# A fused decoder layer on one core: one head in four turned on VectorE and through DRAM instead of on TensorE

## The reference

```
x1  = x  + attention(LN1(x), LN1(x), LN1(x), mask 256x256)      # 16 heads of 32
x2  = x1 + attention(LN2(x1), ctx, ctx, mask per sequence)      # keys and values from ctx
x3  = x2 + gelu(LN3(x2) @ w1 + b1) @ w2 + b2                    # 512 -> 2048 -> 512
out = x3 + batchnorm(W @ y(x3, ctx))                            # non-local block, 128 channels

attention: softmax(q k^T / sqrt(32) * mask - 10000 (1 - mask)) v, then an output projection
```

## Time and profile before

| | |
|---|---|
| median of 3 runs | 2041.2 us |
| lowest, highest | 2039.52, 2042.16 us |
| span of the profiled execution | 2038.2 us |
| busy: PE / DVE / ACT / POOL | 2018.1 / 1447.7 / 1166.7 / 450.6 us |
| granted clock of TensorE, mean | 0.997 |
| DMA | 332469 packets, 190.25 MB; q1 32.5% of 16 engines' span |

### The profile page before, as it was taken

The page is one execution under the profiler, slowest core; times in us unless marked ns, Lnnn a source line. Parts: engine busy times, 40 slices in busy tenths (PEclk is TensorE's granted clock), DMA queues, the critical chain, the costliest instruction groups (busy, mean ns, idle before and its releaser), DMA issues. The chain is left out here.

```text
span 2038.2 us, 41730 instructions
## 1 busy us (share of the span) xinstructions
PE 2018.1 (99%) x14096; PEld 1621.0 (80%) x14096; DVE 1447.7 (71%) x3874; ACT 1166.7 (57%) x3239; POOL 450.6 (22%) x434
## 2 busy tenths in 40 slices
PE   9999999999999999999999999999999999999998
PEld 8877777777777777777777776788888888888887
DVE  7798988888889888888888898565344443435333
ACT  4388888888888888787788888522111121212111
POOL 1011111111113242222232233053031331313000
PEclk9999999999999999999999999999999999999999
DMA  8513243243144344344334334432212212121201
GB/s 270 171 35 77 83 119 77 64 113 97 48 141 133 109 134 109 85 121 126 86 111 123 95 108 120 138 99 70 80 33 77 46 62 72 41 77 46 64 24 47
DMA packets 332469, 190.25 MB, mean 93 GB/s; under 512 B 210688, under 2 KB 276864, under 8 KB 332288
## 3 DMA queue, kind: packets, MB, share of 16 engines
q1 hardware_dynamic: 332288, 187.97, 32.5%
HBM read 137.00 MB, written 50.86 MB: 92 GB/s over the span
## 5 line engine op out<-in xcount | busy, mean ns | idle before, releaser
L1279 ACT ACTIVATE A_p<-A_p,A_nmax 128x256 f32<-128x256 f32 x1024 | 509.1, 506 | 0.0
L1564 DVE TENSOR_TENSOR A_p<-A_sc,A_mk 128x1024 f32<-128x1024 f32 x256 | 312.7, 1221 | 109.1 <-PE A_tp L1046 108.9
L1574 DVE CUSTOM_DVE_ANT_0 A_p<-A_p,A_ma 128x256 f32<-128x256 f32 x1024 | 374.5, 423 | 5.2
L1285 ACT ACTIVATE A_pt<-A_tp 128x512 f32<-128x512 f32 x512 | 276.9, 592 | 142.2 <-PE A_tp L1046 141.8
L1046 PEld LDWEIGHTS A_tp<-A_ident,A_p 128*128 128x128 f32 x2048 | 230.1, 141 | 71.8 <-issue 44.1
L1046 PE MATMUL A_tp<-A_ident,A_p 128*128 128x128 f32 x2048 | 274.2, 277 | 2.0 <-ACT A_pt L1285 1.6
L1279 ACT ACTIVATION_READ_ACCUMULATOR A_p<-A_p,A_nmax 128x1 f32 x1024 | 202.8, 198 | 0.0
L1414 ACT ACTIVATE A_mk<-A_tp,A_cols 128x512 f32<-128x512 f32 x62 | 42.7, 689 | 269.0 <-PE A_tp L68 269.0
L766 POOL TENSOR_TENSOR A_res<-A_res,A_o_bias 128x512 f32<-128x512 f32 x64 | 84.9, 1338 | 473.1 <-DVE A_nmax L1574 281.3
L1414 ACT ACTIVATE A_ma<-A_tp,A_cols 128x512 f32<-128x512 f32 x62 | 42.8, 690 | 242.4 <-PE A_tp L68 242.4
L66 PE MATMUL A_banks<-A_xt_h,A_w_h 128*128 128x512 f32 x384 | 161.3, 420 | 0.9 <-DVE A_res L1543 0.5
(11 more groups left out here) (245 smaller groups left out, 4856.4 us busy)
## 6 DMA issues: line engine op xcount, KB each, us to landing
A_x<-x SPq DMA_DIRECT2D x96, 256.0 KB, 3.6
A_res<-x SPq DMA_DIRECT2D x64, 256.0 KB, 2.9
A_rt<-inverses SPq DMA_DIRECT2D x512, 32.0 KB, 1.8
x<-A_res SPq DMA_DIRECT2D x64, 256.0 KB, 3.2
turned<-A_x SPq DMA_DIRECT2D x240, 64.0 KB, 2.3
inverses<-A_turned_inv SPq DMA_DIRECT2D x512, 1.0 KB
A_e<-ctx_t SPq DMA_DIRECT2D x16, 512.0 KB, 3.9
A_xt_l<-turned SPq DMA_DIRECT2D x16, 512.0 KB, 4.0
```

The lines of the kernel that those rows point to most:

```text
L1279: act.activation(p[:, g % 2, j, t, :], p[:, g % 2, j, t, :], ACT.Exp, scale=-1.0, bias=nmax[:, g % 2, j, t:t + 1], accum_out=rsum[:, g % 2 ...
L1285: act.activation(pt[:, j, :, :], tp[:, j % 2, :].rearrange("p (c s) -> p c s", c=TPB), ACT.Copy)\
L1564: dve.tensor_tensor(p[:, g % 2, heads, :, :].rearrange("p j t s -> p j (t s)"), sc[:, heads, :], m, ALU.mult)\
L1574: dve.tensor_tensor_reduce(out=a_, in0=a_, in1=ma[:, b, t, :], scale=-1.0, scalar=BIG, op0=ALU.add, op1=ALU.min, accum_out=nmax[:, g % 2, ...
```

## The change

MOVED = 1 head of each group, head 0, is no longer turned by TensorE. VectorE transposes its exponentials in 32x32 blocks in place (`exponentials_in_blocks`, one instruction of 128x512, in the slot in which they are made, after `scaled`). SP then writes them to a DRAM tensor in four DMAs, each of 32 partitions by 16 blocks of 32 floats (`store_exponentials`, between `store_inverses` and `load_inverses`), and at the start of the next slot reads them back with keys on the partitions in one DMA of 256 KB (`load_exponentials`, in runs of 128 floats), once the product that last read `pt` is done. TensorE turns heads 1, 2 and 3: two at the slot's start, one inside the first unit; `weigh` waits for the load as well. The first half of the mask now waits for the stores of the slot before, and for one turned head in place of two. ScalarE makes the first two exponentials at the slot's start, ahead of the copies, and has three copies in place of four. In `weighed` it now adds the bias into `cx` in place and then rounds `cx` into `ct_h`, two instructions; the lower part `ct_l` is made by GpSimd, after `until_maxima`, and no longer by VectorE.

```diff
+MOVED = 1
+TURNS = HPG - MOVED
...
@@ -538,6 +541,28 @@
+            def store_exponentials(r, h):
+
+                grp, _, g = group(r, h, 0)
+                sp.wait_ge(p_blk, grp + 1)
+                wait(sp, ld_p, (grp - 1) * DMA)
+                keys = p_dram[g % 2].rearrange("j t (b i) q -> i (j t b) q", i=32)
+                for n in range(P // 32):
+                    rows_ = slice(n * 32, (n + 1) * 32)
+                    own = p[rows_, g % 2, 0:MOVED, :, :].rearrange("i j t (b q) -> i (j t b) q", q=32)
+                    sp.dma_start(keys[:, :, rows_], own).then_inc(st_p, DMA)
+
+            def load_exponentials(r, h, pv):
+
+                grp, _, g = group(r, h, -1)
+                if grp == 0:
+                    sp.wait_ge(w_lo, 3 * KT)
+                else:
+                    sp.wait_ge(done, pv[1])
+                sp.wait_ge(st_p, (grp + 1) * (P // 32) * DMA)
+                sp.dma_start(pt[:, 0:MOVED, :, :].rearrange("p j a (b q) -> p (j a b) q", q=P),
+                             p_dram[g % 2].rearrange("j t (c p) q -> p (j t c) q", p=P)).then_inc(ld_p, DMA)
@@ -596,10 +621,14 @@
 
             def slot(r, k, h, a_, b_, own, pv):
                 if own:
+                    load_exponentials(r, h, pv)
                     store_inverses(r, h)
                     if h == 6 and 0 < k < NU:
                         for t in range(2):
                             load_res(k - 1, r - 1, t + 2)
+                if exists(k, h, 0):
+                    store_exponentials(r, h)
+                if own:
                     load_inverses(r, h)
...
+            def weighed(r, k, h):
+                grp, _, g = group(r, h, -2)
+                b, f = g // KT, g % KT
+                part = slice(b * S, (b + 1) * S)
+                wait_apart(pool, c_hi, grp + 1)
+                pool.tensor_tensor(ct_l[:, f, part], cx[:, :], f32(ct_h[:, f, part]), ALU.subtract).then_inc(c_lo, 1)
@@ -849,6 +885,8 @@
                     upper_context(k + 1, r + 1, 2)
                 if h != 2 or 0 < k < NU:
                     until_maxima(r, k, h)
+                if exists(k, h, -2):
+                    weighed(r, k, h)
...
-            def turn(r, k, h, j):
+            def turn(r, k, h, i):
                 grp, _, g = group(r, h, -1)
-                if NG * k + h - LAG - 1 == 0 and j == 0:
+                n, j = grp * TURNS + i, MOVED + i
+                if grp == 0 and i == 0:
                     pe.wait_ge(pgt_ok, B)
                     pe.wait_ge(m1_ok, B)
                 pe.wait_ge(exped, grp * HPG * TPB + (j + 1) * TPB)
-                wait(pe, pt_ok, grp * HPG + (j - 1))
-                if j < 2 and h in (0, 7) and k == (h == 0):
-                    pe.wait_ge(x_lo, (r + (h == 7)) * TT + (j + (3 if h == 0 else 1)))
+                wait(pe, pt_ok, n - 1)
+                if i < 2 and h in (0, 7) and k == (h == 0):
+                    pe.wait_ge(x_lo, (r + (h == 7)) * TT + (n % 2 + (3 if h == 0 else 1)))
                 for t in range(TPB):
                     for c in range(TPB):
-                        last = pe.transpose(tp[:, j % 2, c * S + t * P:c * S + (t + 1) * P],
+                        last = pe.transpose(tp[:, n % 2, c * S + t * P:c * S + (t + 1) * P],
                                             p[:, g % 2, j, t, c * P:(c + 1) * P], ident[:, :])
                 last.then_inc(turned, 1)
+            def turned_keys(j, c):
+
+                return pt[:, j, :, c * P:(c + 1) * P] if j < MOVED else pt[:, j, c, :]
 
             def weigh(r, h, bank):
                 grp, blk, g = group(r, h, -1)
                 b, f = g // KT, g % KT
                 occupy(bank, cx_ok, NG, h - LAG, r)
-                pe.wait_ge(pt_ok, (grp + 1) * HPG)
+                pe.wait_ge(pt_ok, (grp + 1) * TURNS)
+                pe.wait_ge(ld_p, (grp + 1) * DMA)
                 pe.wait_ge(v_ok, blk * TT + (b + 1) * TPB)
                 for c in range(TPB):
                     for j in range(HPG):
                         rr = slice(j * HD, (j + 1) * HD)
                         last = pe.matmul(banks[rr, bank, 0:S], v[:, b * TPB + c, f * P + j * HD:f * P + (j + 1) * HD],
-                                         pt[:, j, c, :], start=(c == 0), stop=(c == TPB - 1))
+                                         turned_keys(j, c), start=(c == 0), stop=(c == TPB - 1))
                 last.then_inc(done, 1)
...
                 if own:
-                    turn(r, k, h, 2)
-                    turn(r, k, h, 3)
+                    for i in range(2, TURNS):
+                        turn(r, k, h, i)
...
-            def turned_out(r, h, j):
+            def turned_out(r, h, i):
                 grp, _, g = group(r, h, -1)
-                act.wait_ge(turned, grp * HPG + (j + 1))
-                act.activation(pt[:, j, :, :], tp[:, j % 2, :].rearrange("p (c s) -> p c s", c=TPB), ACT.Copy)\
+                n = grp * TURNS + i
+                act.wait_ge(turned, n + 1)
+                act.activation(pt[:, MOVED + i, :, :], tp[:, n % 2, :].rearrange("p (c s) -> p c s", c=TPB), ACT.Copy)\
                     .then_inc(pt_ok, 1)
 
             def weighed(r, k, h):
                 grp, _, g = group(r, h, -2)
                 b, f = g // KT, g % KT
                 act.wait_ge(cx_ok, grp + 1)
-                act.activation(ct_h[:, f, b * S:(b + 1) * S], cx[:, :], ACT.Identity,
-                               bias=bias_sum[:, layer(k, h, -2), 2, f:f + 1]).then_inc(c_hi, 1)
+                act.activation(cx[:, :], cx[:, :], ACT.Identity,
+                               bias=bias_sum[:, layer(k, h, -2), 2, f:f + 1]).then_inc(c_sum, 1)
+                act.wait_ge(c_sum, grp + 1)
+                act.activation(ct_h[:, f, b * S:(b + 1) * S], cx[:, :], ACT.Copy).then_inc(c_hi, 1)
+                first = TPB * MOVED
+                if now:
+                    for n in range(first):
+                        exponential(r, h, n)
                 if own:
-                    for j in range(HPG if bare else 2):
-                        turned_out(r, h, j)
-                if now:
-                    exponential(r, h, 0)
-                    exponential(r, h, 1)
+                    for i in range(TURNS if bare else 2):
+                        turned_out(r, h, i)
                 if leaves and not late(k, h):
                     weighed(r, k, h)
+                if now:
+                    exponential(r, h, first)
                 if own and not bare:
-                    turned_out(r, h, 2)
-                    turned_out(r, h, 3)
-                if now:
-                    exponential(r, h, 2)
+                    for i in range(2, TURNS):
+                        turned_out(r, h, i)
                 unit_out(a_, k)
                 if now:
-                    exponential(r, h, 3)
-                    exponential(r, h, 4)
+                    for n in range(first + 1, 5):
+                        exponential(r, h, n)
                 if even is not None:
                     rows_turned(r + (k < NU), even, tp[:, 0, :])
                     rows_turned(r + (k < NU), odd, tp[:, 1, :])
@@ -1559,7 +1607,10 @@
                         dve.wait_ge(m_ok, blk * 2 - (14 - b))
                     else:
                         dve.wait_ge(m_ok, 1)
-                wait(dve, turned, (grp - 2) * HPG + 2 * (part + 1))
+                if heads.start < MOVED:
+                    wait(dve, st_p, (grp - 1) * (P // 32) * DMA)
+                if heads.stop > MOVED:
+                    wait(dve, turned, (grp - 2) * TURNS + heads.stop - MOVED)
                 m = mk[:, b, :, :].rearrange("p t s -> p (t s)").unsqueeze(1).to_broadcast([P, 2, TPB * S])
                 dve.tensor_tensor(p[:, g % 2, heads, :, :].rearrange("p j t s -> p j (t s)"), sc[:, heads, :], m, ALU.mult)\
                     .then_inc(masked, 1)
@@ -1583,20 +1634,19 @@
                 wait_apart(dve, inv_ok, grp + 1, st_i, (grp - 1) * (P // 32) * DMA)
                 dve.transpose(turned_inv[:, g % 2, :], rinv[:, g % 2, :]).then_inc(inv_t, 1)
 
+            def exponentials_in_blocks(r, h):
+
+                grp, _, g = group(r, h, 0)
+                dve.wait_ge(exped, grp * HPG * TPB + MOVED * TPB)
+                own = p[:, g % 2, 0:MOVED, :, :].rearrange("p j t s -> p (j t s)")
+                dve.transpose(own, own).then_inc(p_blk, 1)
+
             def scaled(r, h, pv):
                 grp, _, g = group(r, h, -2)
                 dve.wait_ge(done, pv[1])
                 dve.wait_ge(ld_i, (grp + 1) * HPG * DMA)
                 wait(dve, c_lo, grp)
                 dve.tensor_tensor(cx[:, :], banks[:, pv[0], 0:S], rt[:, :], ALU.mult).then_inc(cx_ok, 1)
-
-            def weighed(r, k, h):
-                grp, _, g = group(r, h, -2)
-                b, f = g // KT, g % KT
-                part = slice(b * S, (b + 1) * S)
-                dve.wait_ge(c_hi, grp + 1)
```

(20 more changed lines are left out.)

## The result

The time is **2122.4 us** (median of 4 runs, 2121.78 to 2126.38) against 2041.05 for the kernel before (4 runs, 2039.52 to 2042.16) on the same chip: a ratio of 1.040, 95% interval 1.0386 to 1.0415. The change costs 81 us. The forecast was 7 us less than before.

What follows compares the result with a forecast made beforehand. TensorE, busy 99% of the span, was taken as the bound. Terms: -64 saved, +54 for SP's backlog, +3 for body 15 and drain: -7 on 2038.2, so 2031, plus 3.0 carried over: 2034. Own range 2019 to 2048; whole range 1986 to 2068.

Steps and rivals of the forecast that it cites:

- the sum of SP's backlog and what follows from it: SP's full queue at h = 4 to 6 and resulting lateness: 3.9 us a body, 54 in 14 bodies.
- TensorE, 64 us: One head's turning leaves TensorE in each of 128 groups, 0.50 us each: 64 us saved, slots of 8.8 us.
- SP, wait of 2.4 us at h = 6: In bodies 1 to 14 SP's backlog delays head 0's load, so TensorE waits 2.4 us before `weigh`.
- The timetable: SP's entries summed from the start of h = 4: h = 6's load issued at 24.4 us, 6.8 into its slot.
- rival (a): SP's backlog never reaches `weigh`: 1980 us, or 1990 if VectorE's full slots set the pace; chance 0.20.
- h = 7 and after, 1.1 + 0.4 us: The mask waits for late stores, VectorE ends late, TensorE loses 1.1 us; VectorE's longer h = 0 and 1 add 0.4.
- rival (b): The 2.4 us gap at h = 6 halves TensorE's clock: 23 us more, 2057, or 2072 if nothing is covered; chance 0.31.
- The 1.9 us taken as the point: Gap length on TensorE at about which rival (b)'s fall of the clock to half was said to be decided.
- VectorE, 0 to 10 us: VectorE gains a 0.69 us transpose and loses 0.49, +0.20 us a slot: nothing to 10 us, taken as nothing.
- ScalarE nothing: One 0.59 us copy goes, a second pass of at most 0.51 comes: -0.1 to +0.1 us a slot, covered by waits.
- GpSimd nothing: GpSimd's subtraction at the slot's end is wanted only later; costs 1 us, once, at the drain.
- the slack count: VectorE waits only 0.52 to 0.69 us before a full slot's mask, 1.57 after a light one; absorbing idle is gone.

Runs made afterwards that it cites:

- no_transfer: Changed kernel without head 0's stores and loads through DRAM and the waits for them (that head's result left out): 2009.8 us, ratio 0.985.
- tiles_on_act: Changed kernel with the stores of the x tiles issued by ScalarE's queue instead of SP's: 2047.6 us, ratio 1.0043.
- one_pass: Kernel of chunks_on_pool with ScalarE's single pass kept and GpSimd adding the bias and subtracting: 2049.9 us, ratio 1.004.
- chunks_on_pool: Kernel of tiles_on_act with the loads of the weight chunks, 256 KB each, on GpSimd's queue: 2043.8 us, ratio 1.0023.
- split_only: Kernel before, with ScalarE adding the bias in its own pass and GpSimd instead of VectorE making the lower half; no transfer: 2050.7 us, ratio 1.0053.
- filler: Changed kernel with 32 identity transposes on TensorE ahead of the wait in h = 6: 2118.8 us, ratio 1.040.
- split_one_pass: Kernel before, with ScalarE's single pass kept and GpSimd adding the bias and subtracting for the lower half: 2050.3 us, ratio 1.0049.
- load_first: Changed kernel with head 0's load for h = 6 issued in SP's queue ahead of x tile 2: 2131.0 us, ratio 1.046.

## Why the prediction was wrong

The mechanism was the one forecast: TensorE's saving against a backlog in SP's queue that reaches `weigh` at h = 6, then the mask at h = 7. **The step that failed is the sum of SP's backlog and what follows from it**, 54 us forecast and about 94 measured at h = 6 and 7 alone (49 of the 54 were for these). The saving on the other side was put 13 us too high, and two parts costed at nothing were not free.

- **TensorE, 64 us: 51.** By the row of weight loads a head was 0.50 us. From the last matmul ahead of the turns to the first behind them it was 557.00 to 558.03 for eight transposes before; for the four that are left it is 0.59 (509.12 to 509.71, in no_transfer). Half of the work took away 0.44, not 0.50: a part of the 1.03 stays however many turns there are. The slots say 0.40.
- **SP, wait of 2.4 us at h = 6: about 4.2.** The timetable counts from two nominal slots ahead of h = 6, here 508.46 - 17.80 = 490.66 (h = 4 itself began 0.45 us earlier, its slot was 9.35). By that count it held within 0.1 us up to the stores of the exponentials of h = 4. Then the load of the inverses took 2.85 us to issue, not 1.8, and the first tile of h = 5 3.15, not the 2.3 allowed; the load went out 8.8 us into its slot (517.24 less 508.46), not 6.8. The landing itself was no cause: `weigh` started 3.2 us after the issue, 3.4 was taken. What the two rows have beyond their allowance is one issue each, of 1.43 and 1.53 us, where their neighbours took 0.43 to 0.55. Such single issues are in every kernel (52 of over 0.8 us on SP in the kernel before from 115 to 1300 us, 86 in the changed one, with 1543 and 2034 issues). New is where they fall: the load of the inverses at h = 4, now directly behind the stores of the exponentials, has one of 0.9 to 1.9 us in 13 of 15 bodies (12 of 15 in tiles_on_act, with room in the queue; none before and in no_transfer). So the issue times of the earlier trace rows were carried over into another order of entries, where two of them are longer by about 1 us. What makes a single issue long is open; that they vary stood under rival (a), as a reason for less alone.
- **h = 7 and after, 1.1 + 0.4 us: 2.1 at h = 7.** The mask did wait for the stores. I had the last of them land 2.1 us into h = 7; the queue was 2 us later than that timetable, and in the body shown the mask waited 7.1 us.
- **The clock, rival (b): right as a mechanism, wrong as a price.** In the changed kernel 0.50 came after every gap of 2.7 us or more in the bodies. The 1.9 us taken as the point does not hold as one: the clock stayed at 1.00 after a gap of 2.02 us in one_pass (at 694.04) and of 3.13 in chunks_on_pool (at 1303.93), and was 0.50 for the 2 us after one of 1.65 in split_only (at 1264.7). Its 23 us were some 4 (filler), since TensorE had to wait for VectorE anyway. In the prediction 1.1 us of VectorE's lateness covered a part of it; the true cover was larger. By the Trainium skill's TensorE: Matmul & The Clock Gate, HAM oscillation, the start at half rate in every round was to be expected, and the trace agrees for the gaps that came (0.50 from 520 to 524, after 3.99 us); the loop that it describes waits longer for its DMA than the 2.4 us forecast, so the prediction leaned on it more than it bears. The time here didn't hang on it.
- **Rival (a), no backlog, 1980 to 1990:** even without the whole transfer it is 2010, so the change could have gained 30 us at most and not 51 to 61. With room made in SP's queue by moving entries elsewhere it was 2047.6 and 2043.8, no gain at all.
- **VectorE, 0 to 10 us, taken as nothing; ScalarE nothing; GpSimd nothing.** Together they are the 20 us that no_transfer lacks; how they share them is shown in part only. At h = 0 TensorE waits for VectorE in most bodies, as the slack count allowed. ScalarE's second pass costs some 6 us, the slots of h = 1 and 3, where ScalarE keeps its fourth copy (split_only, against split_one_pass, where they are back at 9.30); its busy share of 55% didn't show that `q`'s upper half stands right behind it and that VectorE and then TensorE wait for that. How much of the 20 it is in the changed kernel isn't settled: one_pass took the pass away and was not faster.
- **What the range missed:** the forecast's own upper end, 2048, came from one microsecond more of landing; the issue times, on which both stalls hang, had no allowance upward. A stall at h = 6 and the lateness at h = 7 come from one and the same queue, so they are wrong together: 2 us more of issue time gave 1.8 us more at h = 6 and 1.0 more at h = 7, some 40 us in 14 bodies.

Not settled: what makes up all of the 26 us by which chunks_on_pool is longer than no_transfer in these bodies. The waits named above are some 9 of them.

## What to carry to other kernels

A DMA that is hidden by its bytes (3.4 us in a slot of 9) may not be hidden by its place: SP issued its entries in order, and 0.3 to 0.5 us for each of them (1 to 2 for some) is time of that queue, to be summed like that of a compute engine, in the fullest stretch and not in the mean. When a queue of many small issues is full, moving one entry ahead only moves the wait (load_first); moving sixteen of them to ScalarE's queue removed 75 of 81 us (tiles_on_act). Even so no version that makes the transfer was faster than the kernel before: what TensorE saves in a slot is gained only where the other engines and the queue keep up with the shorter slot too. Ahead of costing an extra pass at nothing because an engine is half idle, read what stands directly behind it in that engine's order and who waits for that.

## What the runs showed of the hardware

- Issuing one store of 512 short pieces kept GpSimd for 2.47 us in the median (0.66, and 1.8 in which nothing else is issued), against 0.50 on SP and 0.53 on ScalarE. 28 loads of 256 KB on GpSimd's queue did no harm that shows (chunks_on_pool).
- Single issues on SP take 0.8 to 2.5 us where their like take 0.3 to 0.5: 86 of 2034 in the changed kernel's bodies, 52 of 1543 before.
- 32 transposes of the identity in a gap of 4 us kept the granted clock at 1.00, where it fell to 0.50 without them.
- `maxima` on VectorE takes 418 to 428 ns in the mean in the kernels before, after, split_only and chunks_on_pool, and 448 and 438 in the two (split_one_pass, one_pass) where GpSimd has a second pass. The Trainium skill, SBUF — State Buffer, Who interferes with whom, has a VectorE instruction with two SBUF inputs, as `maxima` has, contend with a GpSimd instruction that reads SBUF, over a shared pair of ports that is locked and not divided. The trace agrees: the longer mean is made of the 51 and 36 `maxima` that take over 500 ns, the one shown above is 1.50 us long beside GpSimd's subtraction, and the rest take their 418 and 415 ns.
- The same is seen on GpSimd. Its subtraction of 128x256 takes 737 ns in the median in the changed kernel, somewhat more than half of the 1290 of 128x512; the mean of 927 comes from 26 of 128 that took 1.5 to 1.8 us. The bias addition takes 926 in the median, 1082 in the mean.
